# Weight pieces of a two-layer decoder: all prepared first on ScalarE and VectorE, or all but four later on GpSimd

## The reference, cut to what matters

```python
x = ln(x + L0_attn(x))          # 16 heads of 16, scores from "splats" of q and k
x = ln(x + L0_xattn(x, ctx))    # cross attention to the context
x = ln(x + L0_ffn(x))           # top 1 of 8 experts, each 256 x 256
x = ln(x + L1_attn(x))          # causal attention, 16 heads of 16
x = ln(x + L1_xattn(x, ctx))    # two blocks: self and cross attention of 16 heads of 32, each with an MLP of 1024
x = ln(x + L1_ffn(x))           # 16 experts of 64, the best 4 weighted
```

## Time and profile before

| what | us |
|---|---|
| three runs | 3958.79, 3960.23, 3975.51 (median 3960.23) |
| the profiled execution | 3954.29 |
| its span, first to last instruction | 3952.6 |
| TensorE's mean granted clock | 0.895 of full speed |

### The profile page before, as it was taken

The page is one execution under the profiler, slowest core; times in us unless marked ns, Lnnn a source line. Parts: engine busy times, 40 slices in busy tenths (PEclk is TensorE's granted clock), DMA queues, the critical chain, the costliest instruction groups (busy, mean ns, idle before and its releaser), DMA issues. The chain is left out here.

```text
span 3952.6 us, 94629 instructions
## 1 busy us (share of the span) xinstructions
PE 3343.7 (85%) x38960; PEld 2374.8 (60%) x38960; DVE 2807.9 (71%) x6362; ACT 2094.5 (53%) x4222; POOL 975.9 (25%) x1808
## 2 busy tenths in 40 slices
PE   1889888989898888888988888899888898988886
PEld 1666565666565656656656656566655665655554
DVE  5777776777776767777776667677776677777664
ACT  4745565455556554564564555645555556455551
POOL 0312341122222321131132222212342112124310
PEclk9989888988898889888988988898988898989887
DMA  5000000000000000000000000000000000000000
GB/s 163 3 3 2 2 3 4 9 7 3 2 2 2 8 3 7 7 3 2 7 2 2 5 4 7 6 4 2 1 2 3 9 9 4 2 2 2 1 4 6
DMA packets 30365, 31.49 MB, mean 8 GB/s; under 512 B 8673, under 2 KB 26482, under 8 KB 29938
## 3 DMA queue, kind: packets, MB, share of 16 engines
q1 hardware_dynamic: 29938, 25.44, 2.1%
HBM read 21.24 MB, written 4.19 MB: 6 GB/s over the span
## 5 line engine op out<-in xcount | busy, mean ns | idle before, releaser
L1103 ACT ACTIVATE p<-bank,p_log 128x512 f32<-128x512 f32 (+2 forms) x1280 | 746.8, 583 | 1331.3 <-PE bank L797 1266.6
L1669 POOL TENSOR_TENSOR prob<-p,prob 120x256 f16<-120x256 f32 (+2 forms) x512 | 455.5, 890 | 1742.4 <-ACT prob L1104 1741.3
L1104 ACT ACTIVATE prob<-bank,p_log 128x512 f16<-128x512 f32 (+2 forms) x1280 | 747.3, 584 | 0.0
L1368 DVE TENSOR_REDUCE negm<-bank 128x2 f16<-128x512 f32 (+1 forms) x1280 | 675.3, 569 | 33.9 <-PE bank L752 18.2
L1286 DVE TENSOR_TENSOR prob<-p,prob 128x512 f16<-128x512 f32 (+2 forms) x768 | 474.0, 624 | 188.9 <-ACT prob L1104 178.8
L774 PE MATMUL bank<-q,k 32*128 32x256 f16 (+2 forms) x6144 | 496.8, 289 | 65.1 <-issue 34.7
L668 PE MATMUL bank<-w_exp,ident_h 128*128 128x512 f16 x1280 | 429.3, 421 | 32.3 <-DVE negm L1368 15.2
L1678 POOL TENSOR_SCALAR_AFFINE_SELECT probm<-prob 128x128 f16<-128x128 f16 x1024 | 325.9, 358 | 340.4 <-DVE prob L1286 340.4
L774 PEld LDWEIGHTS bank<-q,k 32*128 32x128 f16 (+1 forms) x6144 | 307.9, 110 | 142.7 <-issue 66.8
L797 PE MATMUL bank<-ident_h,negm 128*128 128x256 f16 (+2 forms) x2560 | 384.9, 273 | 0.0
L1661 POOL TENSOR_TENSOR rstd<-veps,minus_half 128x2 f32<-128x2 f32 (+1 forms) x208 | 149.7, 720 | 887.9 <-DVE veps L1261 887.3
(11 more groups left out here) (300 smaller groups left out, 6286.5 us busy)
## 6 DMA issues: line engine op xcount, KB each, us to landing
x<-in_x SPq DMA_DIRECT2D x16, 256.0 KB, 2.7
out<-z SPq DMA_DIRECT2D x16, 256.0 KB, 2.2
xa<-in_li SPq DMA_DIRECT2D x9, 256.0 KB, 4.6
x<-in_li SPq DMA_DIRECT2D x7, 256.0 KB, 4.3
z<-in_wq SPq DMA_DIRECT2D x4, 256.0 KB, 4.4
z<-in_li SPq DMA_DIRECT2D x4, 256.0 KB, 4.1
cx<-in_ctx_t SPq DMA_DIRECT2D x16, 60.0 KB, 1.8
cx<-in_ctx SPq DMA_DIRECT2D x16, 60.0 KB, 1.8
```

Source lines behind the costliest of these rows:

```text
L1103: act(p32[0:n, g % PBUF32, 0:cols], ps[0:n, 0:cols], ACT.Exp, bias=p_log[0:n, :], scale=a.scale)
L1104: act(prob[0:n, 0, g % PBUF, 0:cols], ps[0:n, 0:cols], ACT.Exp, bias=p_log[0:n, :], scale=a.scale).then_inc(a_done, one(a_done))
L1368: v.tensor_reduce(negm[:, h * NT:(h + 1) * NT], ring_v[bank_of(e, v_full)][:, :].rearrange("p (t n) -> p t n", t=NT)[:, :, 0:ATTNS[k].keys ...
L1669: g.tensor_tensor(prob[0:n, 1, m % PBUF, 0:cols], p32[0:n, m % PBUF32, 0:cols], prob[0:n, 0, m % PBUF, 0:cols], ALU.subtract).then_inc(pp_ ...
```

## The change

The first block prepares only the first four pieces. They are fetched ahead of the small loads; ScalarE and VectorE treat them as before. The x tiles are no longer staging buffers (five are left, xa and z), so that the first three x and contexts are fetched in the first block, behind the small loads. In the second block GpSimd takes one piece at the end of each of the first 57 steps (`later_chunk`, `weights_on_pool`): it scales the piece into the high part, scales the staging buffer in place, waits for itself, and subtracts. SyncE's list gets the fetches of these pieces, each behind a wait for the low part of five pieces before. TensorE waits, ahead of the first product with a weight, for that weight's last low part (`weights_made`). The filler products read `w_qkv0` instead of `w_exp`, in the same shape.

```diff
-STAGING = 8
+STAGING = 5
+AT_ONCE = 4
...
-        buffers = x + xa + z
+        buffers = xa + z
...
+            made_with[w.name] = len(chunks)
...
+        def fetch_weights(e, n):
+            _, src, tiles, cols = chunks[n]
+            if n >= STAGING:
+                e.wait_ge(low_made, n + 1 - STAGING)
+            e.dma_start(staging(n, tiles, cols), src).then_inc(staged[n % STAGING], 16)
...
+        def weights_on_pool(e, n):
+            parts, _, tiles, cols = chunks[n]
+            e.wait_ge(staged[n % STAGING], 16 * (n // STAGING + 1))
+            nc.gpsimd.tensor_scalar(parts[:, 0], staging(n, tiles, cols), W_SCALE, None, ALU.mult)
+            nc.gpsimd.tensor_scalar(staging(n, tiles, cols), staging(n, tiles, cols), W_SCALE, None, ALU.mult
+                                    ).then_inc(high_made, 1)
+            e.wait_ge(high_made, n + 1)
+            nc.gpsimd.tensor_tensor(parts[:, 1], staging(n, tiles, cols), parts[:, 0], ALU.subtract
+                                    ).then_inc(low_made, 1)
...
+        def later_chunk(step):
+            n = AT_ONCE + step // PAIR
+            return range(n, min(n + 1, len(chunks)))
...
             @block.sync
             def _(e):
+                for n in range(AT_ONCE):
+                    fetch_weights(e, n)
                 load(e, 0, cen[:, 0], io["centers"].rearrange("(t p) d -> p t d", p=P))
...
-                for n, (_, src, tiles, cols) in enumerate(chunks):
-                    if n >= STAGING:
-                        e.wait_ge(low_made, n + 1 - STAGING)
-                    e.dma_start(staging(n, tiles, cols), src).then_inc(staged[n % STAGING], 16)
+                for b in range(LANES):
+                    e.dma_start(x[LANE[b]][:, :, :], rows_of(io["x"], b)).then_inc(x_in[LANE[b]], 16)
+                for b in range(LANES):
+                    e.dma_start(cxT[LANE[b]], io["ctx_t"][b]).then_inc(c_in[LANE[b]], 16)
...
-                for n, (parts, _, tiles, cols) in enumerate(chunks):
-                    e.wait_ge(staged[n % STAGING], 16 * (n // STAGING + 1))
-                    nc.scalar.activation(parts[:, 0], staging(n, tiles, cols), ACT.Copy, scale=W_SCALE
-                                         ).then_inc(high_made, 1)
+                for n in range(AT_ONCE):
+                    weights_high(e, n)
...
-                for n, (parts, _, tiles, cols) in enumerate(chunks):
-                    e.wait_ge(staged[n % STAGING], 16 * (n // STAGING + 1))
-                    e.wait_ge(high_made, n + 1)
-                    v.scalar_tensor_tensor(parts[:, 1], staging(n, tiles, cols), W_SCALE, parts[:, 0],
-                                           ALU.mult, ALU.subtract).then_inc(low_made, 1)
+                for n in range(AT_ONCE):
+                    weights_low(e, n)
...
-                        mm(ps[:, :], ident_h[:, :], w_exp[:, 0, 0:2, :].rearrange("p t n -> p (t n)"),
+                        mm(ps[:, :], ident_h[:, :], w_qkv0[:, 0, 0, 0:512],
...
+                def weights_made(ws):
+                    if made_with.get(ws.name, 0) > waited[0]:
+                        waited[0] = made_with[ws.name]
+                        e.wait_ge(low_made, waited[0])
...
                     for m in range(1, TURNS):
                         turn("gpsimd", between, n, m)
+                    for w in later_chunk(n):
+                        weights_on_pool(e, w)
...
-                for b in range(LANES):
-                    fetch_x(b)
-                for b in range(LANES):
-                    fetch_ctx_t(b)
-                for (chain, stage), _ in sorted(PLACE.items(), key=lambda item: item[1]):
+                fetched = AT_ONCE
+                for (chain, stage), at in sorted(PLACE.items(), key=lambda item: item[1]):
+                    while fetched < len(chunks) and (fetched - STAGING - AT_ONCE + 1) * TURNS <= at:
+                        fetch_weights(e, fetched)
+                        fetched += 1
```

More of the change, by code:

```diff
@@ L405, in staging @@
             return flat[:, 0:tiles * cols].rearrange("p (a b) -> p a b", b=cols)
-        chunks = []
+        chunks, made_with = [], {}
         def add_weight(w, src, first=0):
@@ L688, in to_xT @@
                     transposes(src, KT, *what, by=by, after=after, meanwhile=STREAM_NORM)
+                waited = [AT_ONCE]
+                def weights_made(ws):
+                    if made_with.get(ws.name, 0) > waited[0]:
+                        waited[0] = made_with[ws.name]
+                        e.wait_ge(low_made, waited[0])
                 def feature_major(ws, col, tiles, src, n_in, n_tok, *what, by="act", low=None):
+                    weights_made(ws)
                     if by == "act":
@@ L1742, in fetch, with fetch_x, fetch_ctx_t @@
                     e.dma_start(dst, src).then_inc(sem, 16)
-                def rows_of(t, b):
-                    return t[b].rearrange("(t p) f -> p t f", p=P)
-                def fetch_x(b, last=None):
-                    if last is not None:
-                        e.wait_ge(*moved("x", last))
+                def fetch_x(b, last):
+                    e.wait_ge(*moved("x", last))
                     fetch(x[LANE[b]][:, :, :], rows_of(io["x"], b), x_in[LANE[b]])
-                def fetch_ctx_t(b, last=None):
-                    if last is not None:
-                        e.wait_ge(*moved("yT", 4, last))
+                def fetch_ctx_t(b, last):
+                    e.wait_ge(*moved("yT", 4, last))
                     fetch(cxT[LANE[b]], io["ctx_t"][b], c_in[LANE[b]])
```

13 lines of the change are left out of this document (added).

## The result

The changed kernel takes 3999.2 us in the median of four runs, the one before 3961.95 us in the median of four on the same chip: 1.0083 of it, 95% interval 1.0055 to 1.0111. **It is slower by 0.8%.** The profiled execution took 3997.47 us, 43 us more than the one before.

What follows compares the result with a forecast made beforehand. No single owner bounds the kernel; TensorE is busy 85% of the span. The start's -42.9, GpSimd's gaps +16 and VectorE's waits +5 sum to -22 us: 3932 us profiled, 3938 us as median, range 3915 to 3982 us.

Steps and rivals of the forecast that it cites:

- The start: Before the first row maxima: 57 of 61 weight pieces leave, TensorE starts at 29.15 instead of 72.06 us, 42.9 us gained.
- since one input makes it most like the selection: GpSimd's scaling of 512 columns priced from selection rows: 0.62 us, upper bound 1.155 us, so a piece takes 2.5 us.
- the count of gaps: GpSimd's idle time between 57 low parts against a 2.75 us piece: 35 of 56 too short, 24 us left beyond slack.
- The discount of a third: First 57 steps: two thirds of the 24 us lateness counted, as TensorE idles 26 us anyway; 16 us lost.
- VectorE's waits: First seven phases: VectorE held by GpSimd at shared SBUF access, 32 us in all, a sixth on the path, 5 us.
- GpSimd becomes the bound: Rival: scalings at 1.155 us make a piece 3.9 us; net +14 to +37 us, up to 3997 us; chance 0.18.
- The point from which it decides: Piece length on GpSimd, about 3.3 us, from which the undiscounted loss is 43 us and the start's gain is used up.
- GpSimd is off the path: Rival: pieces hidden in GpSimd's idle time at 23% share, only the start counts; 3917 to 3922 us; chance 0.22.
- The shared access bites: Rival: all 32 us of VectorE's waits land on the path, 3965 us, or half of them, 3949 us; chance 0.20.
- The covers named as costing nothing: Weights made at least 10 steps before use, fetches issued five pieces ahead: new waits and fetches add no time.
- GpSimd close to 85% busy: Sign of being right: GpSimd's busy share between the first and the 57th step.
- the second rival: GpSimd becomes the bound through dearer scalings: +14 us, or +37 us with all gaps counted, middle given as 3982 us; chance 0.18.

Runs made afterwards that it cites:

- scale_by_tile: The changed kernel with both GpSimd scalings made as products of two tensors, the second a repeated column of 64s; 3996.56 us, 1.0082 of before.
- before_spare: The kernel before, with GpSimd also making a piece's three instructions on unused tiles in each of the first 57 steps; 4070.18 us, 1.0262 of before.
- one_scaling: The changed kernel with the in-place scaling left out of GpSimd's 57 pieces; 3957.23 us, 0.9993 of before.
- act_and_dve: The changed kernel with the 57 deferred pieces made by ScalarE and VectorE, none by GpSimd; 3943.52 us, 0.9958 of before.
- act_and_pool: The changed kernel with ScalarE doing both scalings of each deferred piece and GpSimd only the subtraction; 3949.22 us, 0.9964 of before.
- act_and_dve_4_fillers: act_and_dve with four filler products instead of two in each of the first 57 steps; 3937.67 us, 0.9924 of before.

## Why the prediction was wrong

It said 3938 us (3915 to 3982) and faster or the same; measured were 3999.2 us and slower by 0.8%.

**The start: right.** Predicted 29.15 us for TensorE's first transposes and 42.9 us gained; measured 29.2 and 42.8. A term of it: the first weight's low part starts at 26.92 us (26.77 predicted).

**The failed step: "since one input makes it most like the selection", 0.62 us for a scaling.** It takes 1.49 us, and even the upper bound, the two-input subtraction's 1.155 us, lay under it. This term of the sum was mis-sized; that GpSimd's gaps are too short for a piece, and that TensorE and ScalarE then wait for its low part, was borne out. The row chosen was of another operation with the same number of inputs, and I took "more inputs" as an upper bound without a row that ties the time to them. scale_by_tile shows the tie is not there: two inputs took 1.12 us, one input and a constant 1.49 us. With it a piece is 4.1 to 4.4 us instead of 2.75, and the count of gaps gives 84 us at 4.2 instead of 24. The 769 ns that the Trainium skill gives ("GPSIMD Engine Reference", 3.1 Elementwise) are not borne out for this instruction either: 1483 to 1490 ns from the shortest to the median, for `w_li` from xa.

**The discount of a third: wrong too.** "I take two thirds", since TensorE is idle 26 us anyway. With all of it counted the changed kernel would lose 84 us and before_spare 94; they lost 80.8 and 94.5 (with each piece at its own length the counts are some 87 and 96). At the length that I had predicted, one_scaling lost 40.5 us against 21 predicted (16 + 5) and 26 undiscounted. So had the scaling cost been right, the result would have been no change, not 3938 us. TensorE's idle time did not take up the lateness of others. Why is not tested by itself; my reading is that it is idle because it waits in the same loop.

**VectorE's waits: their amount right, their weight not settled.** I had 32 us of VectorE's time in the stretch; its busy time rose by 29.6 us (190.6 to 220.2), and the mean of its low parts from 611 to 777 ns. (The 559 ns of the earlier trace rows is a median over 256 us; in the stretch alone the medians are 618 and 692 ns.) What of that lay on the path can't be read off, since GpSimd is full there. In one_scaling, of the 14 us beyond the count some five may be the clock, within the scatter; the rest would fit VectorE's waits, but no run parts them. The fills that should have done so had a loss of their own.

**A term left out: the clock.** The prediction named the filler products only for their shape. A wait of TensorE costs the granted clock: in act_and_dve 14 us of 29 came back with the clock. In the changed kernel this term is hidden behind GpSimd.

**The rivals.** It went as "GpSimd becomes the bound", at its far end: I gave +37 us and 3997 us for all gaps counted, at a chance of 0.18, and held that end outside the range. That 3997 us is so near to 3999.2 is in part luck: its scaling was 1.155 us and not 1.49, with 10 us of VectorE's waits added. The point from which it decides (3.3 us a piece) lay too high: with 2.8 us nothing was gained any more, with 3.5 the kernel was 0.8% slower. "GpSimd is off the path" fell with every run that put work there. "The shared access bites" can't be the main cause, as one instruction less on GpSimd gave 40 us back, while VectorE's busy time fell by 6, and act_and_pool came out below its range; a part of the loss may still be its. The covers named as costing nothing held: no wait of TensorE for a weight appears among the waits, and what follows the stretch is longer by 5 us only, less than it differs between executions.

**A sign that did not fit its own sum.** The prediction named "GpSimd close to 85% busy" as a sign of being right. By its own terms it would be 57 x 2.5 + 60 = 202 us of some 276, that is 73% (one_scaling, with the predicted piece, has 202.9 of 291.5). The measured 84% comes with the longer piece and bears nothing out. The middle of the second rival's two ends, +14 and +37 us, is 3985 us and not 3982, which changes nothing here.

**A version that beats both** is act_and_dve_4_fillers: 3937.67 us, 0.9924 of before, interval 0.99 to 0.9948. Its first maxima are 42 us earlier and its stretch is 16 us longer, -26 us, and its median is 30 us under that of before. The fillers alone, in before, gain nothing.

## What to carry to other kernels

Price an operation on a new engine by a row of that operation on that engine, and if there is none let the upper bound of the range reach well past the dearest row at hand, with the result at that bound worked out before the chances are given. For an engine in a loop of two buffers, count the pauses between its recurring duties against the length of the new work, and count them in full: a share of 23% busy hid 56 pauses of 2.1 us in the median, of which eight hold a piece of 4.2 us. The count came near the loss for pieces of that length and was some 15 us too low for the two shorter ones, so more can be lost than it says. Where TensorE may come to wait, look at the granted clock of the steps behind the wait, and try filler products before giving the loss to an engine.

## What was not expected of the hardware

- GpSimd's scaling by a constant of 128x512 float32, to float16 or in place, takes 1.49 us (median; up to 1.93 in the changed kernel); the difference of two tensors of that size 1.15 us; the product with a repeated column 1.12 us.
- VectorE's in-place scaling with two columns is held not by one fill of GpSimd but by a row of them: 0.52 us became 3.4 us beside eight fills of 0.53 us, 3.9 us beside three long ones.
- Fewer products made TensorE busy longer: 2794 in 236.5 us without fillers, 2907 in 225.4 us with them, at granted clocks of 0.76 and 0.94.
